# A two-layer state-space and mixture-of-experts kernel: running sums spread by DMA, and expert rows stored at their tokens' places

## The chip, the cores and the metric

The kernel runs on one core of a Trainium2 chip. The metric is the device time of one execution in microseconds; times are given as the median of repeated runs, lower is better. Five engines work side by side, each through its own instructions in order: PE (TensorE), DVE (VectorE), ACT (ScalarE), POOL (GpSimd) and SP (SyncE, which here only issues DMAs). They wait for each other on semaphores.

## What is computed

Four batches of 1024 tokens with 128 channels go through two layers. Each layer norms and modulates its input, adds a gated attention-like branch, norms and modulates again, and adds a gated mixture of experts. Layer 0's branch is a Mamba scan, layer 1's is a chunked state-space product with four heads; layer 0 picks two experts of eight for a token, layer 1 picks one. What the change touches is this part of layer 1 (cut):

```python
A_cum = jnp.cumsum(A, axis=-1)                     # A = dt * a, negative
L = tril(exp(A_cum[l] - A_cum[s]))
Y_diag = einsum('bcln,bcsn,bhcls,bcshp->bclhp', C, B, L, X)
states = einsum('bcln,bhcl,bclhp->bchpn', B, exp(A_cum[-1] - A_cum), X)
Y_off  = einsum('bcln,bchpn,bhcl->bclhp', C, prev, exp(A_cum))
...
top_idx = jnp.argmax(gate_logits, axis=-1)
for e in range(8):
    h = relu(einsum('bsd,df->bsf', x, w1[e]) + b1[e])
    out = out + (top_idx == e) * (einsum('bsf,fd->bsd', h, w2[e]) + b2[e])
```

## The kernel before

The program is a row of blocks, each ended by a barrier of all engines: `setup`; `mamba` (layer 0's scan); `route` and `sorted_experts` for layer 0; `middle` (layer 0's expert rows gathered and added, the whole of layer 1's branch, and layer 1's second norm); `route` and `sorted_experts` for layer 1; `combine`. `TILES` is 32 tiles of 128 tokens, `BT` is 8 tiles of a batch.

**middle** (from L1242) is one software pipeline written out by hand: rounds b from -3 to 5, eight steps s in each, T = 8b + s. In a round every engine works on several batches at once: POOL gathers layer 0's expert rows for batch b+3, DVE adds them for batch b+2, norms it, and convolves batch b+1, PE projects batch b+1 and runs the scan of batch b, and batches b-1 and b-2 get their last norms. Rounds 0 to 3 run the scan, one tile a step. For tile T of the scan:

- PE `cumulate(T)` (L1454) makes the running sum of the decay, spread over all 128 partitions, in a PSUM bank of its own (two banks `cs`): for each head a matmul of the triangle `tri` with a broadcast column of `dA`. ACT `whole_decay` (L1619) takes its exponential (`cdec`), then PE `mask` (L1477) adds -1e30 before the diagonal to the same bank, and ACT `decay` (L1626) takes the exponential with the negative sum `ncs` as bias (`dec`, four instructions).
- PE `overlap` makes the 128 x 128 product of B and C, DVE `masked` (L1769) copies it to `gm`; POOL `mix` (L1383) multiplies `dec` by it (`mm`), and POOL `weigh_c` (L1376) multiplies `cdec` by C (`cts`).
- PE `outputs` (L1495, L1497) makes y in the single bank `y`, and waits for DVE's `gate` of the tile before it (`yg_done`), which reads that bank. DVE `gate` (L1804, L1810), ACT `square` (L1633), PE `squares` and `narrow` follow.
- DVE `new_state` and `inputs` carry the state and prepare the next tile; PE `turn` transposes for it.

ACT's order in step T is `decay(T)`, `square(T-1)`, `whole_decay(T+1)`, then the readings of the projection banks (`read_piece`), and in step 5 `enter` (four SiLUs and two table loads), in step 6 `gate`. PE's order is `mask(T)`, `outputs(T-1)`, squares, overlap, `new_state(T)`, `turn(T+1)`, `cumulate(T+1)`, the pieces of the projections, `narrow(T-2)`. Which pieces belong to which step is set by `pieces(b, s)`. SP only stores the normed rows of each batch (L1343).

**sorted_experts** for layer 1 (from L1046) goes through 40 slots of 128 rows sorted by expert: POOL gathers a slot's rows by an indirect DMA (L1081, ring of eight, waiting for the transpose eight slots back), PE transposes them (L1090), multiplies by w1 (L1098) and w2 (L1107), ACT applies relu, DVE copies the expert's weights (L1157) and reads the result out with the bias (`read_out`, L1177) into `outs`, two buffers of four slots, and SP stores each group of four in slot order to `ys` (L1194).

**combine** (from L1200) takes the rows back in token order: POOL issues 32 indirect DMAs (L1219) into four buffers of four tiles, DVE multiplies each group of four tiles by the gate (L1228) and adds it to X (L1231), SP stores it to the output (L1237).

`route` for layer 1 makes the table `take` (which token is in which place of a slot, L1030) and loads the experts' weights; its places without a token give row `TOKENS // 2`.

## Time and profile before

| | us |
|---|---|
| median of 3 runs (1279.66 to 1283.87) | 1282.72 |
| profiled execution, its own time | 1281.7 |
| its span from first to last instruction | 1279.9 |
| PE busy / weight load | 922.1 (72%) / 599.0 (47%) |
| DVE busy | 925.9 (72%) |
| POOL busy | 766.5 (60%) |
| ACT busy | 557.9 (44%) |
| scan steps of middle (rounds 0 to 3) | 835.5 to 1094.5 |
| layer 1's experts, first gather to last read-out | 1146.6 to 1229.8 |
| combine, first gather to the end of the span | 1233.4 to 1279.9 |

A row of a group of instructions gives line, engine, operation, output and inputs, count, then busy time and mean duration of one, then the idle time of that engine just before them and what released it. A row of the timeline gives start, duration, engine and line. Busy time of PE counts overlapping matmuls once. PEclk is the granted TensorE clock as a share of its full 2.4 GHz: 1.00 is 2.4 GHz, 0.50 is 1.2 GHz.

### The profile page before, as it was taken

How to read it: one execution, taken by the hardware profiler on the slowest of the kernel's cores; microseconds unless marked ns; L12 is line 12 of the kernel's file. 1: busy time of each engine (PE TensorE's matmuls, PEld its weight loads, DVE VectorE, ACT ScalarE, POOL GpSimd, SP SyncE). 2: the span in 40 equal slices, each digit the busy share in tenths (PEclk: the TensorE clock that was granted, in tenths of full speed). 3: DMA queues.
4: the chain of work that ended last, by engine and by line, in shares of the span. 5: the costliest groups of instructions: out<-in, count | busy, mean ns of one | idle time of the engine just before them, and what ended most of it. 6: DMA issues, size and time to landing. Idle time of an engine off the chain costs nothing. (4 is left out here: it accounts for less than half of the span.)

```text
span 1279.9 us, 15012 instructions
## 1 busy us (share of the span) xinstructions
PE 922.1 (72%) x4480; PEld 599.0 (47%) x4480; DVE 925.9 (72%) x1848; ACT 557.9 (44%) x1166; POOL 766.5 (60%) x493
## 2 busy tenths in 40 slices
PE   3758776977797778674299926697987988519940
PEld 3413323422442243233299923366665767419940
DVE  6439799879997999896877746497794777564522
ACT  1344563466446634541044411626446385206620
POOL 0049598769977998880177648474533527317636
PEclk9879897988898888887599967788987989659975
DMA  6035254334443444413033411100000000042223
GB/s 174 1 119 197 75 170 153 134 119 146 148 142 124 132 148 154 142 50 132 10 81 100 84 54 44 27 17 11 7 1 1 18 1 18 17 171 71 65 61 96
DMA packets 62719, 109.33 MB, mean 85 GB/s; under 512 B 10352, under 2 KB 40112, under 8 KB 62512
## 3 DMA queue, kind: packets, MB, share of 16 engines
q1 hardware_dynamic: 55984, 94.73, 23.1%
q0 software_dynamic: 6656, 13.64, 4.8%
q8 instruction: 37, 0.61, 0.2%
q14 instruction: 42, 0.34, 0.1%
HBM read 94.19 MB, written 14.16 MB: 85 GB/s over the span
## 5 line engine op out<-in xcount | busy, mean ns | idle before, releaser
L684 POOL TENSOR_TENSOR ma_bu<-ma_u,ma_row_b 128x1024 f32<-128x1024 f32 x128 | 305.7, 2400 | 73.5 <-DVE decay_ps L763 46.9
L471 PE MATMUL y_ps<-ma_h,ident 128*128 128x512 f32 x512 | 266.3, 661 | 66.9 <-POOL ma_h L691 46.7
L763 DVE TENSOR_TENSOR_SCAN decay_ps<-decay_ps,ma_bu 128x512 f32<-128x512 f32 x192 | 240.4, 1252 | 46.7 <-ACT decay_ps L589 36.3
L589 ACT ACTIVATE decay_ps<-ma_delta,negA 128x512 f32<-128x512 f32 x256 | 172.5, 687 | 200.6 <-DVE ma_h L773 200.0
L471 PEld LDWEIGHTS y_ps<-ma_h,ident 128*128 128x128 f32 x512 | 103.9, 211 | 216.6 <-issue 115.9
L1081 POOL DMA_INDIRECT s_rows<-xs,take x112 | 124.8, 1114 | 119.5 <-POOLq L846 82.9
L773 DVE TENSOR_TENSOR ma_h<-decay_ps,ma_row_c 128x512 f32<-128x512 f32 x192 | 128.7, 671 | 0.0
L1098 PE MATMUL s_up_ps<-s_xt,s_w 128*128 128x128 f32 x896 | 122.8, 282 | 0.0
L1098 PEld LDWEIGHTS s_up_ps<-s_xt,s_w 128*128 128x128 f32 x896 | 113.4, 198 | 0.0
L1383 POOL TENSOR_TENSOR mi_mm<-mi_dec,mi_gm 128x512 f32<-128x512 f32 x32 | 44.2, 1381 | 106.6 <-issue 74.9
L1353 POOL DMA_INDIRECT mi_y<-ys,where x64 | 65.2, 1019 | 36.0 <-POOLq L1057 18.3
L1107 PE MATMUL s_out_ps<-s_w,s_ht 128*128 128x128 f32 x608 | 86.3, 276 | 0.7 <-DVE s_outs L1174 0.7
L1107 PEld LDWEIGHTS s_out_ps<-s_w,s_ht 128*128 128x128 f32 x608 | 76.5, 192 | 1.0 <-DVE s_ht L1164 0.8
L691 POOL TENSOR_TENSOR ma_h<-ma_h,ma_row_c 128x1024 f32<-128x1024 f32 x32 | 75.3, 2352 | 1.9 <-DVE ma_h L763 1.9
L1157 DVE COPY s_w<-w 128x768 f32 (+1 forms) x112 | 71.4, 642 | 6.6 <-DVE s_outs L1177 2.1
L1125 ACT ACTIVATE s_xt<-s_xt_ps 128x128 f32<-128x128 f32 x112 | 31.7, 283 | 88.0 <-PE s_xt_ps L1090 87.5
L675 POOL TENSOR_TENSOR ma_u<-ma_delta,ma_xp 128x1024 f32<-128x1024 f32 x8 | 19.7, 2460 | 79.9 <-DVE ma_delta L784 79.9
L1425 PE MATMUL mi_pre<-hT,wc 128*128 128x512 f32 x128 | 60.7, 622 | 2.0 <-ACT hT L1568 2.0
L1376 POOL TENSOR_TENSOR mi_cts<-mi_cdec,mi_xbc 128x512 f32<-128x512 f32 x28 | 38.0, 1357 | 34.4 <-ACT mi_cdec L1619 34.3
L1137 ACT ACTIVATE s_ht<-s_up_ps,s_w 128x128 f32<-128x128 f32 x160 | 45.8, 369 | 24.4 <-PE s_up_ps L1098 24.4
L1164 DVE TENSOR_TENSOR s_ht<-s_up_ps,s_act_g 128x256 f32<-128x256 f32 x72 | 30.5, 424 | 28.7 <-ACT s_act_g L1132 28.2
L1219 POOL DMA_INDIRECT c_y<-ys,where x32 | 31.4, 982 | 32.1 <-PEq L1205 22.7
(290 smaller groups left out, 1790.1 us busy)
## 6 DMA issues: line engine op xcount, KB each, us to landing
ma_row_b<-bc_rows SPq DMA_DIRECT2D x64, 512.0 KB, 4.1
ma_row_c<-bc_rows SPq DMA_DIRECT2D x64, 512.0 KB, 5.0
ys<-s_outs SPq DMA_DIRECT2D x28, 256.0 KB
w<-in_experts SPq DMA_DIRECT2D x1, 4112.0 KB, 13.0
w<-in_experts SPq DMA_DIRECT2D x1, 3072.0 KB, 10.5
xs<-rows SPq DMA_DIRECT2D x4, 512.0 KB, 3.2
out<-X SPq DMA_DIRECT2D x8, 256.0 KB, 2.3
s_rows<-xs,take POOLq DMA_INDIRECT x112, 2.7
```

The costliest lines, as they stand in the source:

```text
L471: mm = pe.matmul(y_ps[j][:, col(c)], m.ident[:], h[g % HS][:, col(c)], start=False, stop=True, skip_group_check=True)
L589: act.activation(decay[s % DS][:], delta[b % 2][j][:, col(c)], ACT.Exp, scale=m.negA0[:, j, n:n + 1]).then_inc(decay_done, 1)
L684: pool.tensor_tensor(bu[g % BUS][:], u[b % 2][j][:], row_b[q % BS][:], ALU.mult).then_inc(bu_done, 1)
L691: pool.tensor_tensor(hs[:], hs[:], row_c[q % CS][:], ALU.mult).then_inc(pool_product_done, 1)
L763: dve.tensor_tensor_scan(dst, d[:], bu[g % BUS][:, col(c)], past if c else 0.0, ALU.mult, ALU.add).then_inc(scan_done, 1)
L773: dve.tensor_tensor(h[g % HS][:, col(c)], decay[s % DS][:], row_c[q % CS][:, col(c)], ALU.mult).then_inc(product_done, 1)
L1081: pool.indirect_dma_start(rows[s % ROWS][:], None, m.xs[layer], bass.IndirectOffsetOnAxis(ap=m.take[:, s:s + 1], axis=0)).then_inc(fetched ...
L1098: mm = pe.matmul(up_ps[s % 2][:, f * P:(f + 1) * P], w[s % WS][:, f * P:(f + 1) * P], xt[s % 2][:], start=True, stop=True)
L1107: mm = pe.matmul(out_ps[s % 2][:, 0:P], ht[s % HS][:, f * P:(f + 1) * P], w[s % WS][:, UP + f * P:UP + (f + 1) * P], start=(f == 0), stop= ...
L1157: dve.tensor_copy(w[s % WS][:], m.w[layer][:, bass.ds(expert, 1), :].rearrange("p o f -> p (o f)")).then_inc(copied, 1)
L1353: pool.indirect_dma_start(fetched_rows[G % FETCH][k][:, t, :], None, m.ys[0], bass.IndirectOffsetOnAxis(ap=m.where[:, k, T:T + 1], axis=0) ...
L1425: mm = pe.matmul(bank[:], weights, m.hT[:, n, c * COL + k:c * COL + k + COL], start=(k == taps[0]), stop=(k == taps[-1]))
```

## The change

In `middle`: the matmuls `cumulate` and `mask` and the constants they used are gone. Once a batch, PE makes the running sums of all eight tiles and four heads as rows (`row_ps`, 32 x 128), ACT copies them to SBUF (`row_sb`), and SP stores them to DRAM. In each step SP then loads tile T+2's four rows, broadcast to all partitions (256 KB), into a ring of three buffers `cs`. ACT makes `dec` from it in two stages: `spans`, relu(cum - cs) in four instructions, and `decay`, exp(-x) of 128 x 512 in one; both are now done a step earlier, for T+1. The masking before the diagonal moves into DVE's `masked`, which multiplies by the triangle where it copied. `y` has two banks, so `outputs(T)` waits for the gate of tile T-2. Some pieces and DVE's convolution and first norm move to earlier steps.

In layer 1's experts: POOL issues an indirect store (scatter) for each slot, 12 slots behind the gathers, that puts every row at its token's place in `ys`; `outs` is a ring of 4 x 4 = 16 slots; SP stores nothing there. Empty places go to rows aside, by the table `put` that `route` makes with two more DVE instructions. Empty places now gather a row of zeros kept in the middle of `xs`, and each layer's rows in DRAM step over it.

In `combine`: the 32 indirect gathers become eight direct loads of 256 KB by SP, into a buffer each, at most three in flight.

```diff
-            then(dve.tensor_scalar(m.take[:, 0:slots], take_ps[:], float(TOKENS // 2), None, ALU.add))
+            step_of(dve.tensor_scalar(m.take[:, 0:slots], take_ps[:], float(NOBODY), None, ALU.add))
+            if layer == 1:
+                dve.wait_ge(m.late, LATE[1])
+                then(dve.scalar_tensor_tensor(beside[:], take_ps[:], 0.0, aside[:], ALU.is_equal, ALU.mult))
+                step_of(dve.scalar_tensor_tensor(m.put[:], beside[:], float(NOBODY), take_ps[:], ALU.add, ALU.add))
+            settle()
...
+    OUTS = 2 if layer == 0 else 4
+    LAG = 12
...
-            pool.wait_ge(m.rows_stored, 16 * NBATCH * (layer + 1))
-            for s in range(slots):
+            def gather(s):
                 if s >= ROWS:
                     pool.wait_ge(turned, base + s - ROWS + 1)
                 pool.indirect_dma_start(rows[s % ROWS][:], None, m.xs[layer], bass.IndirectOffsetOnAxis(
                     ap=m.take[:, s:s + 1], axis=0)).then_inc(fetched[s % ROWS], 16)
+
+            def scatter(s):
+                g = s // GROUP
+                pool.wait_ge(out_read, base + s + 1)
+                pool.indirect_dma_start(m.ys[1], bass.IndirectOffsetOnAxis(ap=m.put[:, s:s + 1], axis=0),
+                                        outs[g % OUTS][:, s % GROUP, :], None).then_inc(scattered[g % OUTS], 16)
+
+            pool.wait_ge(m.rows_stored, 16 * NBATCH * (layer + 1))
+            for i in range(slots + (LAG if layer == 1 else 0)):
+                if i < slots:
+                    gather(i)
+                if layer == 1 and i >= LAG:
+                    scatter(i - LAG)
...
-                if t == 0 and g >= 2:
-                    dve.wait_ge(stored[g % 2], 16 * (base // (2 * GROUP) + g // 2))
+                if t == 0 and g >= OUTS:
+                    if layer == 0:
+                        dve.wait_ge(stored[g % OUTS], 16 * (g // OUTS))
+                    else:
+                        dve.wait_ge(scattered[g % OUTS], m.fetches + 16 * GROUP * (g // OUTS))
                 dve.wait_ge(out_done, base + s + 1)
-                dst = outs[g % 2][:, t, :]
+                dst = outs[g % OUTS][:, t, :]
...
-        @block.gpsimd
-        def _(pool):
-            for g in range(GROUPS):
-                if g >= BUFFERS:
-                    pool.wait_ge(x_done, g - BUFFERS + 1)
-                for t in range(g * GROUP, (g + 1) * GROUP):
-                    pool.indirect_dma_start(y[g % BUFFERS][:, t % GROUP, :], None, m.ys[1], bass.IndirectOffsetOnAxis(
-                        ap=m.where[:, 0, t:t + 1], axis=0)).then_inc(fetched[g % BUFFERS], 16)
+        def load(engine, g):
+            first = row_of(g * GROUP * P)
+            engine.dma_start(y[g][:], m.ys[1][first:first + GROUP * P, :].rearrange("(t p) d -> p t d", p=P)
+                             ).then_inc(fetched[g % ways], 16)
 
         @block.vector
         def _(dve):
             for g in range(GROUPS):
-                dve.wait_ge(fetched[g % BUFFERS], before + 16 * GROUP * (g // BUFFERS + 1))
-                ys = y[g % BUFFERS]
-                tiles = slice(g * GROUP, (g + 1) * GROUP)
+                dve.wait_ge(fetched[g % ways], before[g % ways] + 16 * (g // ways + 1))
...
+            for g in range(GROUPS):
+                if g >= ways:
+                    sp.wait_ge(fetched[g % ways], before[g % ways] + 16 * (g // ways))
+                load(sp, g)
...
-        if s == 6 and valid(b + 2):
+        if s == 5 and valid(b + 2):
             out += [("n10", b + 2, 0), ("n10", b + 2, 1)]
-        if s == 7 and valid(b + 2):
-            out += [("raw", b + 2, 2, 0), ("raw", b + 2, 3, 0), ("raw", b + 2, 2, 1), ("raw", b + 2, 3, 1)]
+        if s >= 6 and valid(b + 2):
+            out += [("raw", b + 2, 2, s - 6), ("raw", b + 2, 3, s - 6)]
...
+            def store_rows(n):
+                sp.wait_ge(row_read, n + 1)
+                sp.dma_start(rows[n], row_sb[:]).then_inc(row_stored, 16)
+
+            def load_rows(T):
+                b, t = divmod(T, BT)
+                if t == 0:
+                    sp.wait_ge(row_stored, 16 * (b + 1))
+                before = T - CS
+                if before >= 0:
+                    sp.wait_ge(rel_done, before + 1)
+                    if before % BT > 0:
+                        sp.wait_ge(cdec_done, states(before) + 1)
+                sp.dma_start(cs[T % CS][:].rearrange("p h l -> p (h l)"),
+                             rows[b][t * HEADS:(t + 1) * HEADS, :].rearrange("h l -> (h l)").partition_broadcast(P)
+                             ).then_inc(cs_loaded[T % CS], 16)
+
+            def store_normed(n):
+                sp.wait_ge(modulated11, 2 * n + 2)
+                sp.dma_start(m.xs[1][row_of(n * SEQ):row_of(n * SEQ) + SEQ, :].rearrange("(t p) d -> p t d", p=P),
+                             m.rows[:, tiles(n), :]).then_inc(m.rows_stored, 16)
+
+            for b in ROUNDS:
+                for s in range(BT):
+                    T = b * BT + s
+                    if s == 6 and valid(b + 1):
+                        store_rows(b + 1)
+                    if 0 <= T + 2 < TILES:
+                        load_rows(T + 2)
+                    if s == 4 and valid(b - 2):
+                        store_normed(b - 2)
...
-                pe.matmul(sum_ps, m.ones[:], every, start=True, stop=True).then_inc(sums_done, 1)
+                pe.matmul(sum_ps, m.ones[:], every, start=True, stop=True)
+                wait(pe, row_read, n)
+                pe.matmul(row_ps, every, m.tri[:], start=True, stop=True).then_inc(sums_done, 1)
...
-            def cumulate(T):
-                b, t = divmod(T, BT)
-                pe.wait_ge(dA_done, b + 1)
-                wait(pe, dec_done, T - 1)
-                for h in range(HEADS):
-                    mm = pe.matmul(cs_ps[T % 2][:, h * P:(h + 1) * P], dA[b % 2][:, t, h:h + 1].broadcast_to([P, P]),
-                                   m.tri[:], start=h == 0, stop=True, skip_group_check=h > 0)
-                mm.then_inc(cs_done, 1)
...
-            def mask(T):
-                if T % BT > 0:
-                    pe.wait_ge(cdec_done, states(T) + 1)
-                pe.matmul(cs_ps[T % 2][:], m.identb[:], four(m.past[:]), start=False, stop=True, skip_group_check=True
-                          ).then_inc(mask_done, 1)
...
-                wait(pe, yg_done, T)
+                wait(pe, yg_done, T - 1)
                 for h in range(HEADS):
-                    dst = y_ps[h % 2 * HD:(h % 2 + 1) * HD, h // 2 * P:(h // 2 + 1) * P]
+                    dst = y_ps[T % 2][h % 2 * HD:(h % 2 + 1) * HD, h // 2 * P:(h // 2 + 1) * P]
...
-                act.wait_ge(ncs_done, n + 1)
+                act.wait_ge(sums_done, n + 1)
+                wait(act, row_stored, 16 * n)
+                act.activation(row_sb[:], row_ps, ACT.Copy).then_inc(row_read, 1)
+                act.wait_ge(cum_done, n + 1)
...
-                act.wait_ge(cs_done, T + 1)
+                act.wait_ge(cs_loaded[T % CS], 16 * (T // CS + 1))
                 wait(act, cts_done, T // BT * UPDATES + max(T % BT - 2, 0))
-                act.activation(cdec[T % 2][:].rearrange("p h l -> p (h l)"), cs_ps[T % 2][:], ACT.Exp).then_inc(cdec_done, 1)
-
-            def decay(T):
+                act.activation(cdec[T % 2][:], cs[T % CS][:], ACT.Exp).then_inc(cdec_done, 1)
+
+            def spans(T):
                 b, t = divmod(T, BT)
-                act.wait_ge(mask_done, T + 1)
+                act.wait_ge(cs_loaded[T % CS], 16 * (T // CS + 1))
+                act.wait_ge(cum_done, b + 1)
                 wait(act, m_done, T - 1)
                 for h in range(HEADS):
-                    ins = act.activation(dec[T % 2][:, h, :], cs_ps[T % 2][:, h * P:(h + 1) * P], ACT.Exp,
-                                         bias=ncs[b % 2][:, t, h:h + 1])
-                ins.then_inc(dec_done, 1)
+                    ins = act.activation(dec[T % 2][:, h, :], cs[T % CS][:, h, :], ACT.Relu, scale=-1.0,
+                                         bias=cum[b % 2][:, t, h:h + 1])
+                ins.then_inc(rel_done, 1)
+
+            def decay(T):
+                act.wait_ge(rel_done, T + 1)
+                act.activation(dec[T % 2][:], dec[T % 2][:], ACT.Exp, scale=-1.0).then_inc(dec_done, 1)
...
-                    if valid(b):
-                        decay(T)
+                    if 0 <= T + 1 < TILES:
+                        spans(T + 1)
+                        if (T + 1) % BT > 0:
+                            whole_decay(T + 1)
+                        decay(T + 1)
...
-                dve.tensor_copy(gm[T % 2][:], g_ps).then_inc(gm_done, 1)
+                dve.tensor_tensor(gm[T % 2][:], g_ps, m.tri[:], ALU.mult).then_inc(gm_done, 1)
...
+                    if s < TAPS and valid(b + 1):
+                        convolve(b + 1, s)
...
-                    if s == 5:
+                    if s == 4:
+                        if valid(b + 1):
+                            make_steps(b + 1)
```

Three places show how instructions stand on their engines.

PE, step 4 of a round of the scan, before: the end of the step (`mi_gs` is the shared bank, `mi_cs` the running sum, `mi_pre` a projection piece).

```order
L1461 MATMUL mi_gs<-mi_xbc_3,mi_xbc_2 128x128 [waits mi_silu_done]
L1483 MATMUL mi_gs<-mi_xdd,mi_bt 128x256 [waits mi_xdd_done,mi_bt_done]
L1471 MATMUL mi_tr<-ident,mi_xbc_0 128x128 [waits mi_xdd_done,mi_bt_done,mi_xdt_done,mi_silu_done]
L1471 MATMUL mi_tr<-ident,mi_xbc_1 128x128
L1471 MATMUL mi_tr<-ident,mi_xbc_2 128x128
L1454 MATMUL mi_cs<-tri,mi_dA 128x128 [waits mi_dec_done,mi_dA_done]
L1454 MATMUL mi_cs<-tri,mi_dA 128x128 x3
L1425 MATMUL mi_pre<-hT,wz 128x512 [waits mi_piece_read] x2
L1510 MATMUL mi_o<-wout,mi_yv 128x128 [waits mi_rms_done]
L1510 MATMUL mi_o<-wout,mi_yv 128x128
L1477 MATMUL mi_cs<-past,identb 128x512 [waits mi_cdec_done]
```

And the same place with the change:

```order
L1525 MATMUL mi_gs<-mi_xbc_3,mi_xbc_2 128x128 [waits mi_silu_done]
L1541 MATMUL mi_gs<-mi_xdd,mi_bt 128x256 [waits mi_xdd_done,mi_bt_done]
L1535 MATMUL mi_tr<-ident,mi_xbc_0 128x128 [waits mi_xdd_done,mi_bt_done,mi_xdt_done,mi_silu_done]
L1535 MATMUL mi_tr<-ident,mi_xbc_1 128x128
L1535 MATMUL mi_tr<-ident,mi_xbc_2 128x128
L1496 MATMUL mi_pre<-hT,wz 128x512 [waits mi_piece_read] x2
L1568 MATMUL mi_o<-wout,mi_yv 128x128 [waits mi_rms_done]
L1568 MATMUL mi_o<-wout,mi_yv 128x128
L1553 MATMUL mi_y<-mi_mm,mi_xdt 64x128 [waits mi_s_done,mi_cts_done,mi_yg_done,mi_m_done,mi_xdt_done]
```

The five `mi_cs` matmuls of a step have gone, and with them the waits on `dec_done`, `dA_done` and `cdec_done`; all else keeps its order.

ACT, step 2 of a round of the scan, before:

```order
L1576 ACTIVATE mi_xbc_1<-mi_pre 128x512 [waits mi_piece_done]
L1626 ACTIVATE mi_dec<-mi_cs,mi_ncs 128x128 [waits mi_m_done,mi_mask_done]
L1626 ACTIVATE mi_dec<-mi_cs,mi_ncs 128x128 x3
L1633 ACTIVATE mi_yq<-mi_yv 128x256 [waits mi_o_done,mi_yg_done]
L1619 ACTIVATE mi_cdec<-mi_cs 128x512 [waits mi_cts_done,mi_cs_done]
L1576 ACTIVATE mi_xbc_1<-mi_pre 128x512 [waits mi_piece_done]
```

And with the change:

```order
L1631 ACTIVATE mi_xbc_1<-mi_pre 128x512 [waits mi_piece_done]
L1685 ACTIVATE mi_dec<-mi_cs,mi_cum 128x128 [waits mi_m_done,mi_cum_done,mi_cs_loaded1]
L1685 ACTIVATE mi_dec<-mi_cs,mi_cum 128x128 x3
L1677 ACTIVATE mi_cdec<-mi_cs 128x512 [waits mi_cts_done,mi_cs_loaded1]
L1691 ACTIVATE mi_dec<-mi_dec 128x512 [waits mi_rel_done]
L1696 ACTIVATE mi_yq<-mi_yv 128x256 [waits mi_o_done,mi_yg_done]
L1631 ACTIVATE mi_xbc_1<-mi_pre 128x512 [waits mi_piece_done]
```

The rows for `mi_dec` and `mi_cdec` stand together ahead of `mi_yq`, wait for the loaded ring (`cs_loaded`) where they waited for PE (`mask_done`, `cs_done`), belong to the next tile, and are one instruction of 128 x 512 more.

POOL, layer 1's experts and the block behind, before:

```order
L1081 DMA s_rows<-xs,take 128x128 [waits rows_stored]
L1081 DMA s_rows<-xs,take 128x128 x7
L1081 DMA s_rows<-xs,take 128x128 [waits so_turned] x32
L1057 UNCONDITIONAL_BRANCH
L1213 UNCONDITIONAL_BRANCH [waits barrier_Pool_Activation_PE_DVE_SP_gather]
L1219 DMA c_y<-ys,where 128x128 x16
L1219 DMA c_y<-ys,where 128x128 [waits c1_x_done]
```

And with the change, from the start of the experts:

```order
L1097 DMA s_rows<-xs,take 128x128 [waits rows_stored]
L1097 DMA s_rows<-xs,take 128x128 x7
L1097 DMA s_rows<-xs,take 128x128 [waits so_turned] x5
L1103 DMA ys<-s_outs,put 9217x128 [waits so_out_read]
L1097 DMA s_rows<-xs,take 128x128 [waits so_turned]
L1103 DMA ys<-s_outs,put 9217x128 [waits so_out_read]
L1097 DMA s_rows<-xs,take 128x128 [waits so_turned]
L1103 DMA ys<-s_outs,put 9217x128 [waits so_out_read]
L1097 DMA s_rows<-xs,take 128x128 [waits so_turned]
```

From the thirteenth gather on, each gather is followed by a store; behind the last gather stand 12 stores without a gather, and the gathers of the last block are gone.

## Rows read from the trace of the kernel before

**Rows 1.** Stretches: four rounds of the scan, each engine's busy time, clock, DMA.

```profile
core 0: us, PE busy (x) PEld busy (x) DVE busy (x) ACT busy (x) POOL busy (x), PEclk, DMA share, GB/s
835.50:910.00 74.50, 65.83 (x376) 46.80 (x375) 55.79 (x137) 36.91 (x80) 46.90 (x35) 0.86 0.06 15
910.00:990.80 80.80, 68.54 (x392) 48.40 (x391) 62.95 (x185) 41.64 (x96) 27.80 (x19) 0.84 0.00 1
990.80:1055.20 64.40, 58.48 (x389) 43.52 (x388) 47.58 (x144) 37.07 (x87) 25.24 (x17) 0.90 0.03 9
1055.20:1094.50 39.30, 35.53 (x289) 30.02 (x289) 30.17 (x111) 19.63 (x60) 26.42 (x17) 0.88 0.05 15
```

**Rows 2.** Groups by line, 740 to 1110: busy, mean ns, idle before, releaser.

```profile
L1454 PE MATMUL mi_cs<-tri,mi_dA 128*128 128x128 f32 x256 | 40.5, 311 | 0.0
...
L1626 ACT ACTIVATE mi_dec<-mi_cs,mi_ncs 128x128 f32<-128x128 f32 x128 | 36.4, 367 | 4.5 <-PE mi_cs L1477 3.7
...
L1619 ACT ACTIVATE mi_cdec<-mi_cs 128x512 f32<-128x512 f32 x28 | 16.6, 594 | 25.3 <-PE mi_cs L1454 25.3
...
L1477 PE MATMUL mi_cs<-past,identb 128*128 128x512 bf16 x32 | 14.0, 439 | 20.1 <-ACT mi_cdec L1619 15.3 <-DVE mi_S L1795 4.7
...
L1439 PE MATMUL mi_gs<-mi_dA,tri 128*128 128x32 f32 x8 | 2.1, 349 | 8.0 <-DVE mi_dA L1749 8.0
```

**Rows 3.** Waits, 833 to 1093: who for whom, us in total, times, longest.

```profile
DVE mi_y L1804 <- PE mi_y L1497: 27.5, 9, 7.3
...
DVE mi_gm L1769 <- PE mi_gs L1483: 17.7, 13, 10.7
PE mi_cs L1477 <- ACT mi_cdec L1619: 15.3, 8, 4.6
...
DVE rows L1727 <- ACT mi_rstd_n L1584: 7.1, 2, 6.5
```

**Rows 4.** DMA issues by line: how many, KB each, median us to landing.

```profile
ma_row_b<-bc_rows SPq DMA_DIRECT2D x64, 512.0 KB, 4.1
...
out<-X SPq DMA_DIRECT2D x8, 256.0 KB, 2.3
```

**Rows 5.** Timeline of POOL, layer 1's experts: start, us, line, idle before.

```profile
1146.61 1.02 POOL L1081 DMA_INDIRECT s_rows<-xs,take  x1 [25.08 <-POOLq L846]
...
1158.35 1.11 POOL L1081 DMA_INDIRECT s_rows<-xs,take  x1 [0.30 <-issue]
...
1173.20 1.49 POOL L1081 DMA_INDIRECT s_rows<-xs,take  x1 [0.31 <-PE s_xt_ps L1090]
1175.09 1.43 POOL L1081 DMA_INDIRECT s_rows<-xs,take  x1 [0.40 <-PE s_xt_ps L1090]
```

**Rows 6.** Timeline, first slots of layer 1's experts: PE and DVE.

```profile
1150.91 1.92 PE L1098 MATMUL s_up_ps<-s_xt,s_w 128*128 128x128 f32 x8
...
1152.62 0.42 PE L1090 MATMUL s_xt_ps<-ident,s_rows 128*128 128x128 f32 x1
...
1158.49 1.06 PE L1107 MATMUL s_out_ps<-s_w,s_ht 128*128 128x128 f32 x8
```

**Rows 7.** Timeline, end of the experts and combine, all engines.

```profile
1229.83 0.36 SPq L1194 DMA_DIRECT2D ys<-s_outs  x1
1233.36 0.94 POOL L1219 DMA_INDIRECT c_y<-ys,where  x1 [22.70 <-PEq L1205]
...
1240.36 0.69 DVE L1231 TENSOR_TENSOR X<-X,c_y 128x512 f32<-128x512 f32 x1
...
1273.27 0.94 POOL L1219 DMA_INDIRECT c_y<-ys,where  x1 [0.30 <-issue]
...
1276.51 0.69 DVE L1231 TENSOR_TENSOR X<-X,c_y 128x512 f32<-128x512 f32 x1
```

**Rows 8.** Stretches of 4 us in the scan: PE busy, granted clock.

```profile
887.00:891.00 4.00, 0.75 (x7) 0.94 0.00 0
891.00:895.00 4.00, 2.59 (x18) 0.50 0.05 14
```

125 lines of the change are left out of this document (66 added, 59 removed).

## The prediction

> **What bounds the kernel now.** I read the windows over the scan rounds first, then the groups and waits of that stretch, then the timelines of layer 1's experts and of the last block.
>
> In the four scan rounds (259.0 us) PE is busy 228.3 us, 88%, DVE 196.5 us, ACT 135.3, POOL 126.4 (sums over [rows 1]). DVE's largest waits are for PE: for y 27.5 us, for the shared bank 17.7 [rows 3]. So PE sets the pace, with DVE close behind, above all in rounds 0 and 1 (55.79 of 74.50, 62.95 of 80.80).
>
> In layer 1's experts, PE sets the pace once the rows are ahead: POOL's gathers wait for the transpose and start 1.89 us apart (1173.20, 1175.09 in [rows 5]). In the last block POOL sets it: 32 gathers start from 1233.36 to 1273.27, 1.29 us apart, and only the last group's DVE work and its store stand behind [rows 7].
>
> **The change, part by part.**
>
> *Scan.* PE loses the running sums, 40.5 us, and the mask, 14.0 us [rows 2]. It gains a row matmul a batch; the nearest is the running sum over a batch, 2.1 us for eight records [rows 2], so 2 to 3 us for four batches. PE's work falls to 228.3 - 54.5 + 2.5 = 176 us. Its waits for `cdec` at the mask, 15.3 us [rows 3], go as well: `dec` and `cdec` are made a step earlier, ahead of ACT's long step 5, and PE needs only what POOL makes of them, a step later. The second y bank takes away PE's wait for the gate of the tile just before; that never shows as a large wait, so I put it at nothing. ACT gains an exponential of 128 x 512 a tile; `cdec`'s takes 594 ns [rows 2], so 32 x 0.59 = 19 us, to 154. The four relus stand for four exponentials of the same size and are costed alike. DVE's masking is a multiply where a copy was, also nothing. DVE keeps 196.5 us and becomes the busiest.
>
> The stretch can't fall below 196.5, a gain of 62, and it will not reach it: PE and DVE hand a tile back and forth four times a step, and both are uneven over a round. PE is busy 88% now with the others waiting on it. DVE at 86% gives 229 us: **-30**. Ends: if DVE waits no more than a tenth, 218 (-41, and -50 if it nearly never waits); if the coupling eats most of it, -12. One new coupling is real: DVE's first norm moves from step 5 to step 4, where it must wait for ACT's root of that same step, behind two projection pieces. DVE already waits 7.1 us in two places of this kind [rows 3]; I count it inside the 86%.
>
> The new loads (256 KB a tile, two steps ahead of their use) are nearest to the broadcasts of 512 KB that land in 4.1 us [rows 4]. Two steps are 7.5 us even at DVE's pace of round 3 (30.17 us for eight steps, [rows 1]). Hidden, so nothing. SP's stores of normed rows stand between them; they wait for POOL work of two steps before. In setup two small loads replace two others: nothing. The rounds before the scan keep their bound, POOL's gathers: nothing, within 3 us.
>
> *Route.* Two DVE instructions on the path to the experts: +0.45, at some 0.2 us each with their waits. The small load is queued behind the experts' weights, well ahead of these two; if it came late it would cost its own latency, some 2.3 [rows 4].
>
> *Experts.* POOL now issues 80 indirect DMAs where it issued 40. Alone, one takes 0.94 to 0.95 and the next starts 0.30 later, a pace of 1.25 [rows 5, 7]. Beside DVE's weight copies it is longer: from 1158.35 to 1173.20, eleven starts, the pace is 1.35; in the steady part each lasts 1.43 to 1.49 [rows 5], always beside one copy. So a slot's gather and scatter cost 2.50 alone, 2.7 with the copies at random, 2.98 (1.25 + 1.43 + 0.30) if one of the two always meets the copy. All are above PE's 1.89: **POOL becomes the bound.** I take 2.7, as the two no longer start on PE's transpose. A scatter I price as a gather, since both make one row's worth of addresses for each partition; no row shows it. From below 0.94, as a DMA with 128 row addresses can hardly be cheaper; from above 1.49, the longest gather in these rows, which adds 0.5 x 40 = 20 us.
>
> The Trainium skill (DMA: Bandwidth & Descriptors, section SWDGE vs HWDGE vs iDMA) says that the descriptor rings live in SBUF and that DVE locks GpSimd out of it during its 2-port mode. By that rule the copies cost every meeting and the slot would be at 2.98; the trace agrees only in the steady part, not in the first twenty gathers, so the sum goes by 2.7.
>
> The sum: 12 gathers x 1.35 = 16.2, 28 pairs x 2.7 = 75.6, 12 scatters without copies x 1.25 = 15.0, together 106.8. The last scatter starts at 1146.61 + 0.45 + 106.8 - 1.25 = 1252.6 and lands 2.5 later, as the last gather of the kernel before does (1273.27, its group complete when DVE begins at 1275.8, 0.7 before the row at 1276.51 [rows 7]). The next block begins 1.4 after that, at 1256.5, where it began at 1233.36: **+23** (16 at 2.50 a slot, 31 at 2.98).
>
> *Last block.* 46.5 us now (1233.36 to 1279.9). With it: a first load, between a 256 KB store's 2.3 us and a 512 KB load's 4.1 [rows 4], say 2.8; eight groups of two DVE operations of 0.69 with a handover, 1.46 each [rows 7], 11.7; then the store, 2.7 (1277.2 to 1279.9). Three loads in flight keep ahead of 1.46. Together 17.2: **-29.3**.
>
> Sum: -30 + 0.45 + 22.9 - 29.3 = -36, on the profiled execution's own 1281.7: 1245.7. The median of the runs is 1.0 above that execution, so **1247**.
>
> **The rivals.**
>
> *The scan hardly gains* (DVE takes PE's place at once, with the step-4 wait and ACT's longer queue). For it: DVE is busy 62.95 of round 1's 80.80 us beside 68.54 for PE, so there it has little to give, and a PE with less work may spend more of it at the low clock, which [rows 8] shows behind idle time. Against: 54.5 us of PE work and 15 of waits. At -7 in the scan the time is 1282.7 - 7 - 6 = 1270.
>
> *Slower: the scatter costs POOL more than a gather.* Place: POOL between two gathers; every 0.1 us more is 4 us. It decides from 0.9 us more (36 / 40). If one takes 1.985 (the longest indirect DMA of this kernel, in `middle`), it is 1.03 x 40 = 41 more: 1288.
>
> *Slower: PE falls to 1.2 GHz while it waits for rows.* In the scan the granted clock is 1.00, then 0.94 over a stretch in which PE is busy 0.75 of 4 us, then 0.50 [rows 8]. In the experts PE would idle 0.8 us of each 2.7. At the low level eight matmuls take 1.92 us instead of 1.06 and the transpose 0.42 [rows 6], so a slot is 4.26 us and 40 slots 170: +64, some 1311. It decides from about half the slots at the low level. Against: at that level PE is busy without a gap, after which the clock has risen each time (1150.91 to 1158.49). The Trainium skill (TensorE: Matmul & The Clock Gate, section HAM oscillation) tells of kernels whose clock falls again at every wait for data; by that rule it would be 1311.
>
> *The loads don't hide* (the new ring is late and ACT waits). 1 us a tile is 32 us, the scan's gain gone: 1278.
>
> **How the numbers follow.** Forecast 0.62, own range 1222 to 1262 (scan -50 to -18, experts +16 to +31); scan hardly gains 0.22; costly scatter 0.08; low clock 0.04; late loads 0.04. The range 1222 to 1270 leaves out the last three and part of the edges. A measurement here can tell 0.3% from no change, some 4 us: the first two cases and half of the last are faster, 0.87; same 0.03; slower 0.10.
>
> **What would show it.** Right: no PE group for the running sums, PE busy under 180 us in the scan and DVE above 82%; eight steps of each round shorter; POOL's indirect DMAs back to back from the first gather to the last scatter, about 2.7 us a slot, PE waiting for DMA; a last block of 17 us. Wrong: ACT waiting for the ring's DMA; scatters longer than 1.5 us; PEclk at 0.50 in the experts; a scan over 250 us.

## Result and profile after

The changed kernel takes 1272.3 us (median of 5 runs, 1268.62 to 1272.68) where the kernel before takes 1281.56 beside it: ratio 0.9921, 95% interval 0.9902 to 0.994. It is faster, by 9 us and not by 35, and lies above the range of 1222 to 1270. The span of the profiled execution went from 1279.9 to 1269.8 us. The head of the page of the changed kernel, with the granted clock:

```profile
span 1269.8 us, 14534 instructions
...
PE 901.8 (71%) x4200; PEld 573.3 (45%) x4200; DVE 934.8 (74%) x1850; ACT 577.8 (46%) x1202; POOL 775.3 (61%) x501
...
PEclk9778897988898889787589976888987978659995
```

The 10.1 us between the two spans come out of three stages. The first gather of the experts starts at 1137.09 instead of 1146.61, -9.5, nearly all of it from the scan. From there to the first DMA of the last block (a gather before, a load after) it takes 115.8 us instead of 86.8, +29.0. The last block takes 17.0 instead of 46.5, -29.6.

**The scan.** I measure it from DVE's first `mi_yv` of layer 1 to its 32nd: 843.38 to 1096.92 before, 844.91 to 1087.07 after, -11.3 us. The windows of the two, round by round for the changed kernel, and in one piece for the kernel before:

```profile
core 0: us, PE busy (x) PEld busy (x) DVE busy (x) ACT busy (x) POOL busy (x), PEclk, DMA share, GB/s
844.91:900.99 56.08, 44.96 (x249) 31.00 (x245) 40.76 (x121) 34.01 (x72) 33.91 (x26) 0.85 0.15 40
900.99:981.43 80.44, 61.94 (x333) 42.55 (x334) 64.81 (x185) 48.96 (x113) 34.37 (x21) 0.86 0.11 34
981.43:1046.97 65.54, 56.23 (x325) 39.57 (x324) 52.42 (x144) 42.71 (x97) 29.03 (x18) 0.81 0.15 40
1046.97:1087.07 40.10, 32.76 (x251) 28.21 (x250) 35.20 (x126) 21.88 (x62) 25.11 (x16) 0.77 0.12 35
sum 242.16, PE 195.89 PEld 141.34 DVE 193.20 ACT 147.55 POOL 122.42; mean PE 48.97 PEld 35.34 DVE 48.30 ACT 36.89 POOL 30.60
```

```profile
843.38:1096.92 253.54, 222.92 (x1425) 166.40 (x1425) 191.06 (x577) 133.62 (x316) 119.16 (x82) 0.87 0.03 9
```

PE and DVE are now busy alike, at 81 and 80%. Nobody is near full. The waits of the changed kernel in this stretch, to be held against [rows 3]:

```profile
engine line waited for: us in total, times, longest us
POOL mi_cts L1447 <- ACT mi_cdec L1677: 65.4, 16, 11.5
ACT mi_yq L1696 <- DVE mi_yv L1874: 64.9, 16, 8.6
...
PE mi_gs L1561 <- ACT mi_yq L1696: 15.3, 6, 4.5
...
DVE mi_y L1868 <- PE mi_y L1555: 12.5, 7, 4.0
PE mi_o L1568 <- DVE mi_outs L1888: 12.2, 3, 4.5
...
DVE mi_gm L1833 <- PE mi_gs L1525: 10.5, 4, 3.8
DVE rows L1791 <- ACT mi_rstd_n L1639: 10.5, 3, 5.8
```

DVE's wait for y fell from 27.5 to 12.5, PE's 15.3 for `cdec` is gone, and a new 15.3 stands at its `squares`, for ACT. ACT never waits for the ring's loads (256 KB, landing in 3.3 us). The longest step of the scan, 964.29 to 981.43, got longer (17.1 us, 15.0 before). Its timeline, DVE first, then ACT:

```profile
start us, us, engine line op out<-in xcount [idle before <-releaser]
963.47 0.17 DVE L1786 SCALAR_TENSOR_TENSOR mi_rstd_n<-mi_d 128x8 f32<-128x8 f32 x1
...
964.29 0.42 DVE L1874 TENSOR_TENSOR mi_yv<-mi_y,mi_sz 128x256 f32<-128x256 f32 x1
968.49 0.29 DVE L1833 TENSOR_TENSOR mi_gm<-mi_gs,tri 128x128 f32<-128x128 f32 x1 [3.77 <-PE mi_gs L1525]
...
975.87 4.91 DVE L1791 TENSOR_SCALAR rows<-X,mi_mean_n,mi_rstd_n 128x128 f32<-128x128 f32 x8 [5.79 <-ACT mi_rstd_n L1639]
...
981.43 0.42 DVE L1874 TENSOR_TENSOR mi_yv<-mi_y,mi_sz 128x256 f32<-128x256 f32 x1
```

```profile
958.49 4.27 ACT L1664 ACTIVATE mi_xbc<-mi_xbc,cb 128x1024 f32<-128x1024 f32 x4
962.77 1.28 ACT L1665 ACT_TABLE_LOAD   x1
...
966.29 0.40 ACT L1696 ACTIVATE mi_yq<-mi_yv 128x256 f32<-128x256 f32 x1
966.60 1.05 ACT L1631 ACTIVATE mi_raw<-mi_pre 128x512 f32<-128x512 f32 x2
967.67 1.28 ACT L1671 ACT_TABLE_LOAD   x1
968.96 2.00 ACT L1671 ACTIVATE mi_sz<-mi_sz 128x1024 f32<-128x1024 f32 x2
...
975.39 0.21 ACT L1636 ACTIVATE mi_rstd_n<-mi_rstd_n 128x8 f32<-128x8 f32 x1
```

DVE has the second norm's variance ready at 963.6, and ACT's first SiLU block with its table load ends at 964.05. ACT still comes to the root only at 975.4, since in its list stand the decays of one tile, the square and two readings, then the gate's SiLU block with its two table loads, then the decays of the next tile. DVE idles 5.79 us and then needs 4.91 for its eight rows, which meet POOL's operation of 975.58 (eight such rows take 2.13 at 946.40, with no POOL operation beside them). PE's transposes wait for the rows, and DVE's own next `mi_yv` stands behind them. The same wait, at the same place, was in the kernel before:

```profile
979.19 5.35 DVE L1727 TENSOR_SCALAR rows<-X,mi_mean_n,mi_rstd_n 128x128 f32<-128x128 f32 x8 [6.53 <-ACT mi_rstd_n L1584]
```

**The experts.** The first row below is a scatter among the gathers, the next two are the last scatters; then the three stretches from the first gather to 1247 and the last block:

```profile
1160.42 1.40 POOL L1103 DMA_INDIRECT ys<-s_outs,put  x1 [0.30 <-DVE s_outs L1209]
...
1243.78 0.97 POOL L1103 DMA_INDIRECT ys<-s_outs,put  x1 [0.30 <-issue]
1245.05 0.97 POOL L1103 DMA_INDIRECT ys<-s_outs,put  x1 [0.30 <-issue]
```

```profile
1137.00:1157.00 20.00, 16.43 (x130) 16.02 (x131) 10.49 (x18) 10.93 (x42) 15.64 (x15) 0.83 0.18 48
1157.00:1197.00 40.00, 34.16 (x295) 32.95 (x294) 17.88 (x35) 23.27 (x86) 31.15 (x30) 1.00 0.17 48
1197.00:1247.00 50.00, 31.37 (x259) 29.09 (x257) 12.94 (x28) 20.30 (x73) 38.05 (x37) 0.96 0.20 51
1247.00:1269.00 22.00, 0.00 (x0) 0.00 (x0) 10.44 (x16) 0.00 (x0) 0.00 (x0) 0.50 0.65 191
```

From the first of 80 starts to the last it takes 107.96 us, back to back, with the clock at 1.00 in the middle. Then the end: SyncE waits for the last scatter, then 5.3 us for the barrier of all engines that ends the block, and its first load starts at 1252.85. In the kernel before, SyncE waited 0.5 us for the same barrier, and POOL had issued its last gather 20 us earlier.

```profile
SPq L1233 <- DMA ys<-s_outs,put: 15.1, 1, 15.1
SPq L1073 <- PEq L1073: 5.3, 1, 5.3
```

### The profile page after: what moved, and what is told of

It is laid out like the page before. It is cut to its first block and busy times, and to the rows that moved or that the text cites. A ratio compares the mean times of both kernels' runs of the same rounds, so it can differ in the third digit from the quotient of the medians.

```text
span 1269.8 us, 14534 instructions
## 1 busy us (share of the span) xinstructions
PE 901.8 (71%) x4200; PEld 573.3 (45%) x4200; DVE 934.8 (74%) x1850; ACT 577.8 (46%) x1202; POOL 775.3 (61%) x501
## 5 line engine op out<-in xcount | busy, mean ns | idle before, releaser
L477 PE MATMUL y_ps<-ma_h,ident 128*128 128x512 f32 x512 | 271.7, 672 | 67.2 <-POOL ma_h L697 46.8
L1097 POOL DMA_INDIRECT s_rows<-xs,take x112 | 119.1, 1064 | 116.8 <-POOLq L852 83.2
L1447 POOL TENSOR_TENSOR mi_cts<-mi_cdec,mi_xbc 128x512 f32<-128x512 f32 x28 | 39.7, 1419 | 65.4 <-ACT mi_cdec L1677 65.4
L681 POOL TENSOR_TENSOR ma_u<-ma_delta,ma_xp 128x1024 f32<-128x1024 f32 x8 | 19.7, 2460 | 80.3 <-DVE ma_delta L790 80.3
L1496 PE MATMUL mi_pre<-hT,wc 128*128 128x512 f32 x128 | 65.0, 657 | 3.6 <-ACT mi_raw L1631 2.6
L1209 DVE TENSOR_TENSOR s_outs<-s_out_ps,s_w 128x128 f32<-128x128 f32 x40 | 11.6, 291 | 57.6 <-PE s_out_ps L1136 47.9
L1119 PE MATMUL s_xt_ps<-ident,s_rows 128*128 128x128 f32 x112 | 32.7, 292 | 27.5 <-DMA s_rows<-xs,take 27.5
## 6 DMA issues: line engine op xcount, KB each, us to landing
w<-in_experts SPq DMA_DIRECT2D x1, 3072.0 KB, 10.6
```

What stands on the lines that cost most here:

```text
L477: mm = pe.matmul(y_ps[j][:, col(c)], m.ident[:], h[g % HS][:, col(c)], start=False, stop=True, skip_group_check=True)
L1097: pool.indirect_dma_start(rows[s % ROWS][:], None, m.xs[layer], bass.IndirectOffsetOnAxis(ap=m.take[:, s:s + 1], axis=0)).then_inc(fetched ...
L1496: mm = pe.matmul(bank[:], weights, m.hT[:, n, c * COL + k:c * COL + k + COL], start=(k == taps[0]), stop=(k == taps[-1]))
```

## Experiments

They ran in four sessions on three chips (the second and the fourth on the same one), each session with the kernel before beside it: 1312.8 us in the first, 1319.8, 1311.7 and 1318.4 in the next, against 1281.56 beside the result. Absolute times are compared within a session only. Scan lengths are measured as above, each in one profiled execution. The same scan code ran in five of them: 242.2 us in the result, 239.7 in both repetitions of the changed kernel, 241.4 in `scan_only` and 236.6 in `one_block`. So a scan says something only where it lies clearly outside 236.6 to 242.2. The scan of the kernel before is 253.5 in its profile and 255.6 in `tail_only`.

**The halves, first session.** `scan_only` takes the changed `middle` with the experts and the last block of before; `tail_only` takes `middle` of before with the changed tail.

> The change in the scan alone; layer 1's experts and the last block as before. My theory (the scan gained some 10 us and the rest cancels): 1271 us, 10 to 12 under before, scan rounds 242 us long, experts and last block 86.8 and 46.5 us. Rival (the two halves act on each other, for instance through the clock): it differs from that by over 4 us.

> The scan as before, the scatters, direct loads and their two route instructions alone. My theory: no change within 2 us (1281 to 1284), because 29 us lost in the experts stand against 29.5 won in the last block. Rival (the new tail is worth what I forecast, -6): 1276.

`scan_only` 1297.8, ratio 0.988 (0.9845 to 0.9914), 15 us under the kernel before where 10 to 12 were expected. `tail_only` 1318.9, ratio 1.0047 (1.0028 to 1.0065): alone, the tail loses 6 us here. The profile of the result gives the tail -0.6. The difference is in the experts: from the first gather to the last scatter 122.1 us in `tail_only` (in its slowest execution, 1328.1) and 120.0 and 123.2 in the two repetitions of the changed kernel, 108.0 in the result. The experts of the kernel before are longer there too, but by less: 91.9 us from the first gather to the last block in `scan_only`, 86.8 in the profile ahead of the prediction. This is a wait of POOL in the experts of the changed kernel in the fourth session, and below it what PE does at that time:

```profile
1200.95 1.68 POOL L1097 DMA_INDIRECT s_rows<-xs,take  x1 [1.73 <-remote]
```

```profile
1201.09 2.04 PE L1127 MATMUL s_up_ps<-s_xt,s_w 128*128 128x128 f32 x8 [5.05 <-ACT s_xt L1154]
```

PE has stood idle for 5.05 us, and its next eight matmuls take 2.04 us, as at the low clock, where 1.06 is usual in this stage. The trace of this run has three idle times of PE over 3 us behind the first rows (5.06, 5.05 and 3.19 us); that of the result has none over 2.0. Its clock is 0.76, 0.95 and 0.92 over its first 20 us, the next 40 and the rest, against 0.83, 1.00 and 0.96 in the result. Near its end eight scatters wait for DVE's read-outs, 8.8 us in all, where those of the result stand back to back. In the longest of PE's idle times DVE does nothing either and ACT 1.1 us of work, and no matmul record is missing in the stage (320 at each line, as in the result). What stops them there the trace doesn't name; I leave it open. The gain of the change is that of the scan: the tail gives 0.6 us in the result and costs time in these sessions.

**The order of DVE, first session.** `old_places` puts the convolution, the first norm and the pieces back at their steps of before:

```diff
-                    if s < TAPS and valid(b + 1):
-                        convolve(b + 1, s)
...
+                    if 1 <= s <= TAPS and valid(b + 1):
+                        convolve(b + 1, s - 1)
...
-        if s == 5 and valid(b + 2):
+        if s == 6 and valid(b + 2):
             out += [("n10", b + 2, 0), ("n10", b + 2, 1)]
```

> After, with the projection pieces, the convolution and the first norm in the steps in which they stood before. Theory A (DVE is overloaded in steps 0 to 3 because the convolution now falls together with the expert rows): the scan gets shorter, 3 to 8 us under after. Rival B (the moves were needed to spread PE's and ACT's work in steps 6 and 7): 3 to 8 us over after. If the uneven load does not matter: within 2 us.

1303.8, ratio 0.9919 (0.9902 to 0.9935); scan 243.4. The windows of its scan:

```profile
sum 243.43, PE 196.89 PEld 141.85 DVE 177.63 ACT 148.58 POOL 116.73; mean PE 196.89 PEld 141.85 DVE 177.63 ACT 148.58 POOL 116.73
```

DVE is busy 15 us less than in the changed kernel (6 us of it in the convolutions and 3 in the rows, the same operations made shorter, I take it by meeting less of POOL's work), and the scan isn't shorter: 243.4 against 236.6 to 242.2. Theory A fell. Rival B, 3 to 8 us longer, can't be told from no change. DVE's wait for the root grew meanwhile from 10.5 to 15.5 us. The amount of DVE's work doesn't set the scan.

**The last block joined to the experts, first session.** `one_block` moves loads, gate and sums of the last block into the experts' block, so that SyncE waits for the scatters' semaphores alone.

> After, with the last block's loads, DVE work and stores in the experts' block, so that no barrier stands between the last scatter and the first load. Theory (of the 7.8 us between the last scatter's start and the first load, 2.3 are the landing and 5.3 the barrier, which waits for POOL to finish behind its last DMA): 4 to 6 us under after, about 1267. Rival (SP waits for the writes themselves): within 1 us of after.

1298.5, ratio 0.989 (0.9865 to 0.9916). SyncE's rows at its end; its last scatter starts at 1278.08:

```profile
1280.38 7.58 SPq L1254 DMA_DIRECT2D s_y<-ys  x8
```

The first load comes 2.3 us behind the last scatter's start instead of 7.8, and 19.6 us lie from there to the end of the span instead of 24.8. So the barrier behind POOL's last indirect DMA costs 5 us. The changed kernel as it is did not run beside `one_block`, so the gain is read from these rows and not from the time.

**Second session.** `after_same` is the changed kernel again. `square_first` puts `square(T - 1)` ahead of the spans and decays of T + 1 on ACT. `no_exp` leaves one element of the decays' exponential. `pe_back` gives PE the matmuls of the running sums back, into a bank that nobody reads.

```diff
-                    if 0 <= T + 1 < TILES:
-                        spans(T + 1)
...
                     if 0 <= T - 1 < TILES:
                         square(T - 1)
+                    if 0 <= T + 1 < TILES:
+                        spans(T + 1)
```

```diff
+                for h in range(HEADS):
+                    pe.matmul(spare_ps[HD:P, c:c + P], dA[b % 2][:, t, h:h + 1].broadcast_to([P, HD]), m.tri[:], ...)
```

> The change as it is, as the reference for the runs beside it. It was 0.992 of before; every theory expects that again within 0.3%, with a scan of 242 us of which ACT is busy 148, DVE 193 and PE 196.

> After, with ACT's square of tile T-1 ahead of the three decay stages of tile T+1, where before had one of them behind it. Theory A (the scan is now a chain through ACT, and PE's 15 us of waits for the square are part of it): PE's waits for the square go and the scan is 5 to 12 us shorter. Rival B (the waits only move: the decay stages then wait longer for DVE's gate, which the square needs, and POOL and PE get their products later): within 3 us, or longer.

> After, leaving out the exponential of 128 x 512 that the change added for each tile (it is done on a single element, so the decays are not computed); ACT loses 32 x 0.6 = 19 us. Theory A (ACT's in-order chain bounds the scan in steps 5 to 7): 8 to 19 us shorter. Theory B (DVE bounds the scan, as forecast): within 3 us of after.

> After, with the running-sum matmuls put back on PE at their old place, into a bank that nobody reads (64 instead of 128 output partitions, same moving columns): 40 us of PE work more, no new waits. Theory A (PE is off the path now for most of the scan): 0 to 15 us longer. Rival (PE work still sets the time and the gain came from it one for one): 30 to 40 us longer. If taking 54 us of work away is worth only the 11 us that the change shows, putting 40 back costs about 8.

| | time, us | ratio (95%) | scan, us |
|---|---|---|---|
| after_same | 1304.7 | 0.9888 (0.9855 to 0.9922) | 239.7 |
| square_first | 1325.4 | 1.0042 (1.0015 to 1.0068) | 260.3 |
| no_exp | 1303.3 | 0.9893 (0.9841 to 0.9944) | 236.1 |
| pe_back | 1313.3 | 0.9945 (0.9919 to 0.9972) | 245.9 |

`square_first` halves PE's wait for `mi_yq` (8.6 us for 16.3), and the scan gets 20.6 us longer, because the decays now queue behind DVE's gate. These two of its waits were 65.4 and 62.7 in `after_same`:

```profile
POOL mi_cts L1447 <- ACT mi_cdec L1677: 104.5, 18, 10.8
ACT mi_yq L1696 <- DVE mi_yv L1874: 82.0, 18, 7.6
```

So ACT's place for the decays, a step ahead, is right, and my first theory (that `square`'s place behind them cost the gain) fell. `no_exp` takes 12 us off ACT's busy time, and its scan of 236.1 lies 0.5 below the shortest of the same code: ACT's work spread over the steps isn't the bound either. In `pe_back` the windows of the scan read

```profile
868.35:1114.24 245.89, 214.12 (x1400) 155.50 (x1400) 191.67 (x575) 148.03 (x343) 119.73 (x81) 0.92 0.13 37
```

PE gets some 37 us of matmuls back (232 records of 313 ns), is busy 21 us more than in the repetitions (193.0), its clock goes from 0.84 to 0.92, and the scan is 6.2 us longer (3.7 above the longest of the same code). So taking work off DVE or ACT gains nothing clear, and PE's gives back a sixth of what was added. What is left to try is the order.

**Third session, the chain of steps 5 to 7.**

```diff
 norm_first
+                    if s == 6 and valid(b - 1):
+                        root(rstd["n11"][:], rstd["n11"][:], n11_var, b, logs, n11_rstd)
                     if s == 6 and valid(b + 1):
                         gate(b + 1)
-                    if s == 7 and valid(b - 1):
-                        root(rstd["n11"][:], rstd["n11"][:], n11_var, b, logs, n11_rstd)
 split_silu, in enter(n), the other two in gate(n)
-                for j in (2, 3, 0, 1):
+                for j in (2, 3):
...
 y_one, and PE and DVE use y_ps[0] alone
-                wait(pe, yg_done, T - 1)
+                wait(pe, yg_done, T)
...
```

> The changed kernel with one item of ScalarE's list moved: the second norm's root (two small operations) stands in step 6 ahead of the SiLU of the gate instead of at the end of step 7. Theory (the long step of each round is a chain over the engines: VectorE's variance, ScalarE's SiLU block of 4.6 us, the decays, the root, VectorE's 8 rows, TensorE's pieces): VectorE's wait for the root, 5.8 us in a round, 3 rounds, goes, and the scan's 31 steps take 6 to 14 us less than the 240 of the changed kernel; the time is 0.5 to 1.1% below it. Rival (the steps are set by a resource that is merely met there): within 3 us of it.

> The changed kernel with the six SiLUs of a round on one column of 1024 each; the rest of the SiLUs is left out, so its output isn't the reference's. The four table loads of a round stay. It takes 6.3 us of a round's ScalarE work away, 25 in all, at two places in a row, where leaving out 19 us of exponentials spread over all 32 steps gave 3.6. Theory of the chain in steps 5 to 7: the scan is 15 to 25 us shorter. Rival, ScalarE's work doesn't matter wherever it lies: 5 us or less.

> The changed kernel with two of the four SiLUs of step 5 moved behind the table load of step 6: the same work and as many table loads, the block of step 5 2.1 us shorter, that of step 6 2.1 us longer. Theory of the chain: steps 5 and 6 lie in the same chain up to the root, so the scan changes by less than 3 us either way; the root comes no earlier. If instead the block of step 5 alone sets the long step, 5 to 8 us less.

> The changed kernel with the second output bank taken back: TensorE's outputs of a step wait for VectorE's gate of the step before. VectorE and TensorE then hand over once more in a step. If the second bank carries the gain of the scan (waits of VectorE for y fell from 27.5 to 12.5 us), the scan is 8 to 15 us longer, 250 or more. If the removed running sums carry it: 3 us or less.

| | time, us | ratio (95%) | scan, us |
|---|---|---|---|
| norm_first | 1293.5 | 0.9864 (0.9835 to 0.9892) | 230.9 |
| no_silu | 1287.0 | 0.9802 (0.9766 to 0.9838) | 228.5 |
| split_silu | 1305.4 | 0.995 (0.9932 to 0.9968) | 241.4 |
| y_one | 1302.1 | 0.9928 (0.9907 to 0.9949) | 240.0 |

Two small operations moved by a step take 9 us off the scan (230.9 against 240.0 and 241.4 of `y_one` and `split_silu` beside it). Leaving out most of the SiLUs takes 11 off, less than the 15 to 25 expected, and 8 below the shortest scan of the same code. `split_silu` stays within 3 us, as the chain says. `y_one` shows that the second output bank carries nothing clear of the gain (240.0, inside 236.6 to 242.2).

**Fourth session, side by side.** `before_norm` is the kernel before with the same move of the root; `norm_one_block` joins `norm_first` and `one_block`.

> The changed kernel as it is, so that the next three have it beside them on the same chip. Its scan takes 240 us from the first gate to the last.

> The changed kernel with the second norm's root in step 6 ahead of the SiLU of the gate. Theory of the chain in steps 5 to 7: the scan is 231 us, 9 less than the changed kernel's beside it, and the time 0.5 to 0.9% less. Rival: the difference seen before between two sessions on the chip was the sessions'; within 0.3% of it.

> The kernel before with the same move of the root. Its VectorE waits 7.1 us for the root in all. If the chain through the root was a bound of its own there already, the scan is 5 to 7 us shorter, 0.4% of the time or more. If TensorE's work filled the time beside it (88% busy there), it gains under 3 us, and the wait is one that the change uncovered.

> The changed kernel with the root in step 6 and with the last block's loads, gate and sums in the experts' block, so that SyncE waits for the scatters' semaphores alone and not for the barrier behind them. The two lie in different stages and add up: 9 us less in the scan, 4 to 5 less behind the last scatter, 13 in all, 1.0% below the changed kernel.

| | time, us | ratio (95%) | scan, us | span, us |
|---|---|---|---|---|
| after_again | 1306.6 | 0.9918 (0.9892 to 0.9945) | 239.7 | 1304.5 |
| norm_again | 1300.6 | 0.9864 (0.9821 to 0.9907) | 230.9 | 1292.7 |
| before_norm | 1317.7 | 0.9989 (0.9963 to 1.0014) | 252.9 | 1316.7 |
| norm_one_block | 1295.8 | 0.9834 (0.9795 to 0.9873) | 234.1 | 1292.3 |

The scan's 9 us repeat. With the 234.1 of `norm_one_block` the three scans with the move average 232.0, the five of the changed kernel's scan without it 239.9. The intervals of the times of `norm_again` and `after_again` touch, so for the time alone the gain is likely and not certain; `norm_first` with 0.9864 (0.9835 to 0.9892) and the scan say the same. This is DVE in the same step as above, in `norm_again`, and below it ACT's root:

```profile
983.22 0.42 DVE L1874 TENSOR_TENSOR mi_yv<-mi_y,mi_sz 128x256 f32<-128x256 f32 x1
987.68 0.29 DVE L1833 TENSOR_TENSOR mi_gm<-mi_gs,tri 128x128 f32<-128x128 f32 x1 [4.03 <-PE mi_gs L1525]
...
989.19 2.64 DVE L1791 TENSOR_SCALAR rows<-X,mi_mean_n,mi_rstd_n 128x128 f32<-128x128 f32 x8
...
993.45 0.42 DVE L1874 TENSOR_TENSOR mi_yv<-mi_y,mi_sz 128x256 f32<-128x256 f32 x1
```

```profile
986.74 0.20 ACT L1636 ACTIVATE mi_rstd_n<-mi_rstd_n 128x8 f32<-128x8 f32 x1
...
987.20 1.28 ACT L1671 ACT_TABLE_LOAD   x1
```

The wait of 5.8 us is gone, the rows take 2.64 instead of 4.91, and the step is 10.2 us long instead of 17.1. In the next round the step shortens from 12.3 to 6.9, and the one behind it gives back 5.7 (2.8 to 8.5). So of the 8.8 us between `after_again` and `norm_again`, 5.2 are gained in and behind the step of round 1, nothing in round 2, and 3.9 in steps of the last round, most of it ahead of that round's root: for these the chain is not shown.

In the kernel before the same move gives nothing clear: 0.9989, and a scan of 252.9 against the 253.5 of the profile ahead of the prediction and the 255.6 of `tail_only`. The long step shortens there as well, to 10.6 us from the 14.9 of `tail_only`, and steps behind it get longer. PE is busy 220.4 us of 252.9 there; that its work fills the time is my reading. So the wait was there before, and only with the change does removing it shorten the scan. `norm_one_block` has the lowest ratio of all. Against `after_again` it gains 0.8% and not the 1.0% expected: the 5 us behind the last scatter are there (19.7 to the end of the span against 25.0), but its scan is 234.1 and not 230.9, within what the same code spreads.

## Why the prediction was wrong

- **The scan, forecast -30, measured -11.3: the step that failed.** "DVE keeps 196.5 us and becomes the busiest." and "DVE at 86% gives 229 us". DVE's work was right (193.2 on the stretch measured here, 191.1 before), but it runs at 80%, and taking 15 us of it away (`old_places`) makes nothing shorter. The step took a share of busy time that a near-bound engine had shown (PE, 88%) for what the next one would reach. What sets the longest step instead is a chain over the engines: DVE's variance, what stands in ACT's list up to the root (decays, the gate's SiLU block, decays again), the root, DVE's rows, PE's transposes. The wait at its end was in [rows 3], 7.1 us for `rstd`, and I put it "inside the 86%". With the root moved up the scan is 230.9, which is 9 us of the 19 that the forecast has too much. It isn't the 229 of the prediction, which counts the four rounds of 259.0 us: on the stretch measured here the forecast is 223.5. DVE stays at 80% (185.5 of 230.9) even then. What bounds the rest stays open. The prediction also named -12 as the end "if the coupling eats most of it", close to what came, and then ended its range at -18.
- **PE's work, forecast 176, measured 195.9.** On the stretch measured here, 222.9 less the two groups removed (36.5 and 13.0 there) plus 1.2 for the row sums makes 174.6; 21 us are missing. The groups present in both sum to 226.4 before and 238.3 after, so 12 of them are the same matmuls taking longer, at a mean clock of 0.83 instead of 0.87. The other 9 are an error of the sum: groups overlap, and their busy times add up to more than PE's. All groups sum to 275.9 before, where PE is busy 222.9, and to 239.5 after, where it is busy 195.9. The overlap shrank from 53.0 to 43.6, so the groups removed had run in part beside others, and taking their whole time off PE's busy time took too much. One such group, before and after:

```profile
L1425 PE MATMUL mi_pre<-hT,wz 128*128 128x512 f32 x24 | 11.8, 616 | 0.0
```

```profile
L1496 PE MATMUL mi_pre<-hT,wz 128*128 128x512 f32 x24 | 13.8, 704 | 4.3 <-ACT hT L1623 4.3
```

- **The removed waits.** Right that PE's wait for `cdec` goes and that the second bank is worth nothing clear (`y_one`). Of the scan's gain some 6 us are PE's matmuls (`pe_back`, and 3.7 beyond the spread of the same code). A share of the new order isn't shown (`old_places` is 1.3 beyond it). The remainder wasn't taken apart.
- **The ring's loads, hidden.** Right: ACT waits for none.
- **Experts, forecast +22.9 and 0.45 for the route, measured +29.0.** The mechanism held: POOL is the bound, starts back to back, 107.96 us to the last scatter where 105.6 were forecast. The 28 pairs take 77.7 us, 2.77 a slot and not 2.7. A scatter costs what a gather does (median 0.987 us, lands in 2.3, one of 40 over 1.5), so the rival of the costly scatter is out. The term that was missed is the end: 3.9 us from the last scatter's start to the next block, measured 7.8, and `one_block` takes it to 2.3. The rule of the Trainium skill (DMA: Bandwidth & Descriptors, section SWDGE vs HWDGE vs iDMA), taken to the end, gave 2.98 us a slot; the trace stays below it with 2.77.
- **Last block, forecast -29.3, measured -29.6.** Right, 17.0 against 17.2.
- **The low clock.** With PE idle between slots the clock stays at 1.00 and 0.96 in the result. The Trainium skill (TensorE: Matmul & The Clock Gate, section HAM oscillation) tells of kernels whose clock falls again at every wait for data; the result's experts don't show it at their waits of up to 2.0 us. The experts of the repetitions do, behind PE's idle times of 5 us. In the scan the mean clock fell with PE's work (0.87 to 0.83), and `pe_back` raised it to 0.92. I had counted that in no sum.
- **The rival that came nearest** is the one with 0.22, that the scan hardly gains (-7, 1270). DVE in PE's place was the wrong reason; ACT's longer queue, which it names beside it, is part of the chain. That its total lies 2 us off is in part luck: the scan gained 4 more, and the experts lost 6 more, than it says.

## What to carry to other kernels

When the busiest engine of an in-order pipeline loses work, the next bound need not be the next busiest engine: follow the longest step of a round from engine to engine and price what stands ahead of each hand-off in that engine's list. A wait of a few us whose removal gains nothing under a nearly full engine can be worth removing when that engine empties, and a move of two instructions was then worth 9 us of scan beside the change's own 11; test it in the old kernel and in the new one. Busy times of groups that overlap can't be taken off an engine's busy time one for one. A store or gather moved onto POOL cost its issue time, 1.27 us each here and 1.4 beside DVE's copies, and a barrier behind the last one cost 5 us more, unless the next work waited for its semaphore in the same block. Before a difference of a few us in one stage is explained, look how far that stage differs between runs of the same code, here 5.6 us.

## What the runs showed of the hardware

- A scatter of 128 rows of 512 B took POOL 0.97 to 1.00 us in 33 of 40 cases and up to 1.54 in the others, with 0.30 to the next, as a gather does.
- The barrier behind POOL's last indirect DMA held SyncE 5.3 us after the data had landed (`after`); without it the first load started 2.3 us after the last scatter's start (`one_block`). In the kernel before, with SyncE's own store last, it was 0.5 us. What the barrier waits for isn't in the trace.
- DVE's convolution steps, which read two tensors, got longer when they met POOL's operations: two of them that take 2.47 us alone took 5.41 beside a sum and a product on POOL. All rows are of the changed kernel:

```profile
926.47 5.41 DVE L1802 SCALAR_TENSOR_TENSOR mi_xbc<-mi_raw,tap,mi_xbc 128x1024 f32<-128x1024 f32 x2
...
937.20 2.47 DVE L1802 SCALAR_TENSOR_TENSOR mi_xbc<-mi_raw,tap,mi_xbc 128x1024 f32<-128x1024 f32 x2
```

```profile
926.23 2.35 POOL L1441 TENSOR_TENSOR X<-X,lnb_gate 128x1024 f32<-128x1024 f32 x1
928.54 2.25 POOL L1447 TENSOR_TENSOR mi_cts<-mi_cdec,mi_xbc 128x512 f32<-128x512 f32 x1
```

- Work put back on PE cost less than its duration: 37 us of matmuls (`pe_back`) added 21 us of busy time and 6 of scan, while the mean clock rose from 0.84 to 0.92.
